# Mean of squares beside layer 3, expert banks freed by two engines, VectorE's masks and scans in another order, layer 5's relus on one engine

## The reference, cut to what matters

```python
# 1. mixer: 8 recurrent steps, in two directions
for _ in range(8):
    up   = relu(a + shift_r(up)   @ W2.T + b2)
    down = relu(a + shift_l(down) @ W2.T + b2)
h = relu(c + (shift_r(up) @ W4.T + b4) + (shift_l(down) @ W4.T + b4))
# 2. attention as a gated recurrence over 256 tokens, on layernorm(h)
#    (running maximum of log gates, decayed sums), then an RMS norm of its output
rms = sqrt(mean(out * out, axis=-1) + 1e-8)
h = h + out / rms * norm_scale
# 3. eight experts, each three 64x64 layers, mixed by a softmax over the batch mean
h = h + ffn(layernorm(h))
```

## Time and profile before

| | |
|---|---|
| median of 3 runs | 638.05 us (637.66 to 638.29) |
| the profiled execution: its own time | 636.97 us |
| its span, first to last instruction | 635.2 us |
| outside the span | 1.77 us |
| TensorE busy | 587.7 us, 93% |
| VectorE, ScalarE, GpSimd busy | 436.5, 344.4 and 123.1 us |
| mean granted TensorE clock | 0.967 of full speed |

### The profile page before, as it was taken

One profiled execution on the slowest core, in us unless ns is written; L12 is line 12 of the kernel. 1 busy time (PEld: TensorE's weight loads), 2 busy tenths in 40 slices (PEclk: granted clock), 3 DMA queues, 4 the chain that ended last, 5 costly groups with the idle time before them and its releaser, 6 DMA issues.

```text
span 635.2 us, 11790 instructions
## 1 busy us (share of the span) xinstructions
PE 587.7 (93%) x4731; PEld 229.5 (36%) x4731; DVE 436.5 (69%) x747; ACT 344.4 (54%) x608; POOL 123.1 (19%) x140
## 2 busy tenths in 40 slices
PE   6889998999999999999999999878799999999995
PEld 4323342334334334334334334233443333333331
DVE  2336864893895795797697598496237887776765
ACT  2238363754845854864854864887533344344441
POOL 9200020132113023015015015025011111010100
PEclk9989897999999989999989999999769999999998
DMA  1300000000000000000000000000001212211122
GB/s 41 90 3 2 1 3 0 1 2 3 2 1 3 2 1 3 1 2 4 1 1 1 1 2 2 1 1 1 6 1 18 34 19 33 35 24 27 21 32 33
DMA packets 37432, 7.27 MB, mean 11 GB/s; under 512 B 36405, under 2 KB 36701, under 8 KB 37373
## 3 DMA queue, kind: packets, MB, share of 16 engines
q1 hardware_dynamic: 36301, 5.72, 5.2%
q0 software_dynamic: 768, 0.69, 0.4%
q10 hardware_dynamic: 304, 0.07, 0.0%
HBM read 2.26 MB, written 4.19 MB: 10 GB/s over the span
## 4 chain that ended last, share of the span: by engine, by line
PE 76%; DVE 16%; issue 4%; ACT 3%; POOL 0%; DVEq 0%; POOLq 0%
PE TB L776 15%; PE TB L766 10%; PE QB L1117 7%; PE QB L799 7%; PE TB L893 6%; PE QB L826 5%; DVE M L1342 4%; PE TB L901 3%; PE QB L901 3%; PE QB L819 3%; PE TB L874 3%; PE QB L843 2%; DVE E L1516 2%; PE TB L826 2%; DVE XC_IS L1526 2%
## 5 line engine op out<-in xcount | busy, mean ns | idle before, releaser
L497 ACT ACTIVATE U<-TB 128x512 f32<-128x512 f32 x128 | 69.5, 596 | 132.4 <-PE TB L766 132.4
L776 PE MATMUL TB<-U,w2T 64*64 64x512 f32 x896 | 129.4, 615 | 8.3 <-ACT U L497 4.7
L718 ACT ACTIVATE E<-TB,bn_t 128x512 f32<-128x512 f32 x112 | 70.9, 684 | 92.8 <-PE TB L893 92.8
L1192 DVE TENSOR_SCALAR U<-TB 128x512 f32<-128x512 f32 x128 | 81.9, 681 | 54.1 <-PE TB L766 54.1
L766 PE MATMUL TB<-X,w_in 6*128 6x512 f32 x512 | 73.9, 647 | 2.1 <-DVE fw L1473 0.9
L893 PE MATMUL TB<-XN,fw 64*64 64x512 f32 x512 | 71.2, 611 | 4.0 <-issue 3.6
L776 PEld LDWEIGHTS TB<-U,w2T 64*64 64x64 f32 x896 | 43.5, 137 | 66.7 <-issue 29.5
L1117 PE MATMUL QB<-E,fwo 64*64 64x512 f32 x224 | 58.4, 593 | 2.3 <-DVE XC_IS L1526 1.7
L799 PE MATMUL QB<-XC_IS,wproj 64*64 64x512 f32 x384 | 56.5, 606 | 2.9 <-ACT LI L611 2.7
L1117 PE MATMUL QB<-E,fwo_sw 64*64 64x512 f32 x224 | 57.6, 593 | 0.0
L1516 DVE SCALAR_TENSOR_TENSOR E<-QB,t_neg,AT 128x512 f32<-128x512 f32 x54 | 38.0, 745 | 21.9 <-PE QB L901 21.9
(11 more groups left out here) (241 smaller groups left out, 904.7 us busy)
## 6 DMA issues: line engine op xcount, KB each, us to landing
result<-V SPq DMA_DIRECT2D x64, 64.0 KB, 1.8
X<-in_x SPq DMA_DIRECT2D x32, 8.0 KB
XN<-in_ffn_v SPq DMA_DIRECT2D x2, 256.0 KB, 3.6
XN<-in_ffn_g SPq DMA_DIRECT2D x2, 256.0 KB, 4.6
fw<-in_ffn_W POOLq DMA_DIRECT2D x2, 128.0 KB, 2.9
fw<-in_ffn_W POOLq DMA_DIRECT2D x2, 64.0 KB, 2.6
fwo<-in_ffn_Wo POOLq DMA_DIRECT2D x2, 64.0 KB, 2.6
fwo_sw<-in_ffn_Wo POOLq DMA_DIRECT2D x2, 64.0 KB, 2.3
```

What stands on the lines that cost most here:

```text
L497: nc.scalar.activation(U3[:, 2 * j:2 * j + 2, 1:T + 1], rowsof(TB[j][:, :]), ACT.Relu)\
L718: nc.scalar.activation(H1[i % 2][:, k, :], TB[k][:, :], ACT.Relu, bias=bn_t[:, 0, p:p + 1]).then_inc(b["h1"], 1)
L776: pe.matmul(TB[j][half[r ^ (j % 2)], :], w2T[half[r], D * r:D * r + D], U3[half[r], 2 * j:2 * j + 2, 2 * down:2 * down + T], start=True, s ...
L1192: nc.vector.tensor_scalar(U3[:, 2 * j:2 * j + 2, 1:T + 1], rowsof(TB[j][:, :]), 0.0, None, ALU.max)\
```

## The change

Four edits, all of the order of work or of who does it; the arithmetic stays.

1. In turns with mixer and late part, layer 3 is issued as bank 0, bank 1, the first half of the mean of squares, bank 3, the second half, bank 2; bank 2 is crossed there, and `turned` keeps account of which half holds which direction from then on. VectorE reads the mean of squares before its relus of layer 3 and no longer behind them.
2. The relus of layer 5 all run on ScalarE (`ON_ACT`), in every turn with a mixer; `relu_done` counts the semaphores accordingly.
3. VectorE's list in the middle of a turn: masks 0 and 1, scans 0 and 1, residual sum, masks 2 and 3, (no relu 5), scans 2 and 3, masks 4 and 5, then the normaliser.
4. In the experts VectorE frees only `QB[0]`; ScalarE copies `QB[1]` to a new tile `RQ` after its `h1`; GpSimd adds the two; the transposition comes one pair later. The last block is finished by VectorE alone, as before.

```diff
+ON_ACT = (5,)
+        RQ = [HR[:, 0:512], HR[:, 512:1024]]
+        SWAPPED = {(k, late): (1, 3) for k in range(1, 8) for late in (False, True)}
+        SWAPPED[3, True] = (1, 2, 3)
...
             for F in range(2 * G):
-                after(pool, b["res"], 2 * F - 3)
+                after(pool, b["res"], F - 1)
                 nc.gpsimd.tensor_tensor(rowsof(R1[F % 2]), rowsof(HH[:, HC * F:HC * F + HC]),
                                         BOW.unsqueeze(1).to_broadcast([P, 2, T]), ALU.add).then_inc(b["res_a"], 1)
+                if F > 0:
+                    pool.wait_ge(b["res"], F)
+                    pool.wait_ge(b["res_q"], F)
+                    nc.gpsimd.tensor_tensor(RES[(F - 1) % 2], RES[(F - 1) % 2], RQ[(F - 1) % 2], ALU.add)\
+                        .then_inc(b["res_sum"], 1)
...
-                for j in (0, 2):
+                for j in range(4) if k in ON_ACT else (0, 2):
...
             for i in range(N_PARKED + 1, len(made)):
                 h1(i)
+                F, p = made[i - 2] // EP, made[i - 2] % EP
+                if i > N_PARKED + 1 and p == EP - 1:
+                    act.wait_ge(b["l3_mm"], F + 1)
+                    after(act, b["res_sum"], F - 1)
+                    nc.scalar.activation(RQ[F % 2], QB[1][:, :], ACT.Identity).then_inc(b["res_q"], 1)
...
+            def layer(it, k, buf, late, beside=None):
+                if late and k == 3:
+                    bank_sum(it, k, 0, late)
+                    bank_sum(it, k, 1, late)
+                    for h, j in enumerate((3, 2)):
+                        beside(h)
+                        bank_sum(it, k, j, late)
...
                 if p == 0:
-                    after(pe, b["res"], 2 * F)
+                    after(pe, b["res"], F)
+                    after(pe, b["res_q"], F)
...
-                for j in (1, 3):
+                for j in () if k in ON_ACT else (1, 3):
...
                 nc.vector.tensor_tensor(RES[F % 2], QB[0][:, :], R1[F % 2], ALU.add).then_inc(b["res"], 1)
-                dve.wait_ge(b["res"], 2 * F + 1)
-                nc.vector.tensor_tensor(RES[F % 2], QB[1][:, :], RES[F % 2], ALU.add).then_inc(b["res"], 1)
...
-                if F >= 0 and behind == 1:
+                if F >= 0 and behind == 2:
                     token_major(F)
```

More of the change, by code:

```diff
@@ L254, in build @@
         ahead = {n: sem("ahead_" + n) for n in ("l1_mm", "h1", "l2_mm", "h2")}
+        SWAPPED = {(k, late): (1, 3) for k in range(1, 8) for late in (False, True)}
+        SWAPPED[3, True] = (1, 2, 3)
+        turned = {(j, k, late): sum(j in SWAPPED[i, late] for i in range(1, k)) % 2
+                  for j in range(4) for k in range(1, 9) for late in (False, True)}
         def settle(engine, it, mix, att, late):
@@ L767, in inputs, with bank_sum @@
                               start=(k == 0), stop=True).then_inc(s["mix_mm"], 1)
[L769 to L777, removed]
+            def bank_sum(it, k, j, late):
+                relu_done(pe, it, k - 1, j)
+                for r in range(2):
+                    down = r ^ turned[j, k, late]
+                    pe.matmul(TB[j][half[r ^ (j in SWAPPED[k, late])], :], w2T[half[r], D * r:D * r + D],
+                              U3[half[r], 2 * j:2 * j + 2, 2 * down:2 * down + T], start=True, stop=False)
+            def layer(it, k, buf, late, beside=None):
[5 more added lines that the diff above has]
+                        bank_sum(it, k, j, late)
+                else:
+                    for j in range(4):
+                        bank_sum(it, k, j, late)
                 inputs(it, k, buf)
@@ L943, in turn @@
                 if mix:
-                    layer(it, 1, buf)
+                    layer(it, 1, buf, late)
                 if att:
@@ L954, in turn @@
                 if mix:
-                    layer(it, 2, buf)
+                    layer(it, 2, buf, late)
                 if att and plain:
@@ L976, in turn @@
                 if mix:
-                    layer(it, 4, buf)
+                    layer(it, 4, buf, late)
                 if att and not plain:
@@ L983, in turn @@
                 if mix:
-                    layer(it, 5, buf)
+                    layer(it, 5, buf, late)
                 if late:
@@ L995, in turn @@
                 if mix:
-                    layer(it, 6, buf)
+                    layer(it, 6, buf, late)
                 if late:
@@ L1009, in turn @@
                 if mix:
-                    layer(it, 7, buf)
+                    layer(it, 7, buf, late)
                 if att and not plain:
@@ L1044, in turn @@
                 if mix:
-                    final(it, buf)
+                    final(it, buf, late)
                 if att and not plain:
@@ L1306, in turn @@
                             .then_inc(s["cs_out"], 1)
-                if mix:
-                    relu(it, 3)
                 if late:
@@ L1315, in turn @@
                             .then_inc(s["rms_add"], 1)
+                if mix:
+                    relu(it, 3)
                 if att and not plain:
@@ L1335, in turn, with running_max @@
                     relu(it, 4)
-                if att and not plain:
+                def running_max(ns):
                     dve.wait_ge(s["decay0_out"], a + 1)
                     after(dve, s["nq_out"], 2 * a)
-                    for n in range(SB):
+                    for n in ns:
                         dve.wait_ge(s["g_out"], 2 * a + n // 2 + 1)
@@ L1343, in turn @@
                             .then_inc(s["m_out"], 1)
+                if att and not plain:
+                    scores(a, range(0, 2))
+                    running_max(range(0, 2))
                 if last_late:
@@ L1361, in turn @@
                 if att and not plain:
-                    scores(a, range(0, 4))
+                    scores(a, range(2, 4))
                 if mix:
                     relu(it, 5)
+                if att and not plain:
+                    running_max(range(2, 4))
                 if att and not plain:
@@ L1368, in turn @@
                     dve.wait_ge(s["k_out"], 2 * a + 2)
+                    scores(a, range(4, 6))
                     for c in range(2):
@@ L1374, in turn @@
                         .then_inc(s["nn_first"], 1)
-                    scores(a, range(4, 6))
                     dve.wait_ge(s["lam_out"], a + 1)
```

41 lines of the change are left out of this document (28 added, 13 removed).

## The result

The median went from 637.86 us (four runs, 634.67 to 638.29) to **618.09 us** (four runs, 616.55 to 627.66); the ratio is 0.9692, with a 95% interval from 0.9644 to 0.9741. The prediction was 617.3 us, range 614 to 624. The profiled execution took 616.92 us, its span 615.1. One of the four runs, 627.66 us at a mean granted clock of 0.962 against 0.975 to 0.977 in the others, is not in the ratio.

A forecast was written before the change was run, and what follows sets the result against it. PE was taken as busiest, waiting for VectorE from relu 4 to layer 7 and for `finish` in experts. Terms 11.2 + 1.2 - 0.5 - 0.3 + 1.9 + 7.2 = 20.7 us gave 617.3 us, range 614 to 624.

The forecast's parts named there:

- 0.4 us a turn: Layers 3 to 4: sigmoid directly follows relu 3, so layer 4's inputs come 0.4 us sooner each turn; bounds 0 to 0.86.
- relu 6 starts 1.47 us sooner relative to relu 4: Middle of a turn: VectorE stays gapless, relu 6 moves 1.47 us sooner, and layer 7's inputs still follow 2.59 us later.
- The bounds: Edits 1 to 3, turns 2 to 7: 11.2 us forecast; 2.4 if only the 0.4 comes through, 16 with PE's freed time.
- 1.20 + 0.27: VectorE's list, relu 4 to relu 6: 1.20 us from two relus moved away, 0.27 from a first scan no longer slowed.
- the 1.9 us: Two half-clock stretches behind PE's 1.31 us idle time at the masks vanish, saving 2 x 0.94 us; bounds 0 to 1.9.
- The rival, falls elsewhere: Clock falls remain or two to four come anew around PE's other idle places, 0.94 us each: 619 to 623 us; chance 0.22.
- 0.3 lost: Turn 8, masks ahead of scans waiting for PE's scores, together with the last block's tail: 0.3 us lost.
- 0.5 forecast: Turn 0, mixer only: PE waits for every relu, two more in series on ScalarE cost 0 to 1.08 us; 0.5 lost.
- 7.2 us: Experts: the 0.48 us wait for `finish` vanishes in 15 of 16 blocks, 7.2 us in all; bounds 0 to 7.2.
- The slower rival: Experts: GpSimd's two adds a block hold up VectorE's weighted relus, 34 us more and the 7.2 gone: 658 us; chance 0.03.

The follow-up runs named there:

- e5: Changed kernel without edit 1, mean of squares behind layer 3 again: 627.22 us, ratio 0.9855 to the kernel before; full turns 48.08 us against 47.63.
- e6: Changed kernel with masks 4 and 5 back between the normaliser's first scan and the carry: 619.04 us, ratio 0.9732 to the kernel before; full turns 47.19 us.
- e3: Changed kernel with VectorE's masks and scans in the old order, layer 5's relus still on ScalarE: 625.38 us, ratio 0.9739 to the kernel before; full turns 48.00 us.
- e4: Changed kernel with layer 5's relus on ScalarE and VectorE again, new order kept: 629.08 us, ratio 0.9886 to the kernel before; full turns 48.62 us.
- after_again: Changed kernel measured again, unaltered, on one chip with e8 (repeated) and e9: 626.26 us, ratio 0.9852 to the kernel before.
- e2: Changed kernel with the experts of before (edits 1 to 3 alone): 626.26 us, ratio 0.9858 to the kernel before; full turns 47.62 us.
- e8: Changed kernel with the edits of e6 and e7 together: 617.44 us (ratio 0.9711 to the kernel before), repeated 614.76 us (0.9696); full turns 47.18 us.
- e7: Changed kernel with turn 0's relus of layer 5 on both engines: 620.73 us, ratio 0.9758 to the kernel before; turn 0 33.48 us.
- e9: e8 with the old order of masks and scans in turns without a mixer (turn 8): 614.23 us, ratio 0.9654 to the kernel before.

## Why the prediction was right, and where it was not

**Edit 1**: right in mechanism and size. 0.4 us a turn was put down to ScalarE's wait for projection 2; the wait is gone, 0.45 came, and e5 gives it back.

**Edits 2 and 3**: this step failed: "So VectorE again has no gap, relu 6 starts 1.47 us sooner relative to relu 4." It started 1.00 sooner. The two relus' 1.20 us came and the slow first scan went (0.68 us against 0.93, the pair at 264.75 taking 1.26). What was missed is what masks 4 and 5 did where they stood: they covered the normaliser's scan until the carry could read it, and they came late enough never to wait for their scores. Moved ahead, both joints open, each by 0.18 us (0.10 behind the predecessor's end in place of 0.08 ahead of it). e6 puts them back and gets 1.44 of the 1.47 in the turn. In turn 1 the same step cost 0.4: 47.76, and 47.35 with the masks put back. The bounds ran from 2.4 to 16 us and held it, yet nothing in the text asked what the moved masks had been hiding, though it asked that of everything else.

The Trainium skill (VectorE: DVE Perf Modes, "The DRAIN you can't avoid") says of eight copies, with a semaphore behind each or behind the last alone, that "the semaphore costs nothing extra here". In this case a wait for the predecessor's result does cost: the independent mask of e6 begins 0.08 us before the scan's end, the dependent carry of the kernel after 0.10 behind it. The same section says that an instruction which is not held starts before the pipeline behind the last one is empty; the 0.08 us agree with that.

The text also treated edits 2 and 3 as 1.20 + 0.27, two gains that add. They don't: 0.62 and 0.00 alone, 1.00 together. What the relus save comes through in full only if PE isn't held behind the masks (e3, where PE then sets the stretch), and PE's earlier start is of use only if VectorE's list has got shorter (e4, where PE waits 1.27 us for relu 6).

**The clock**: the 1.9 us came, and the four profiles against ten bear out the reason, PE's 1.31 us of idle time behind the masks; why this gap sets the fall off in one turn and not in the next is not explained by any run, and e4's 1.27 us in another place set off none. The rival, falls elsewhere, was right in turn 8 with one fall, and in executions that were not profiled it may have been right further: 619 to 623 was its price, and five of the six executions of after_again took 622 to 629. In turn 2 a stretch of 6.8 us (98.95 to 105.78 before) was missing from the profile after, 3.3 us that the sum didn't have; e2, whose turns are the same instructions, has it (6.8 us from 97.94, turn 2 57.70), so that it belongs to the execution and not to the change. Without that the span would have shrunk by 16.8 us, 3.9 less than forecast. That the median came within the range is luck in part: of the ten executions of the kernel after on record, 616.55 to 628.61 us, five are above 624.

**Turn 8**: forecast between 1 us either way, 0.3 lost taken; 1.0 was lost. The scans there did get shorter as hoped (3.27 us in two pairs against 4.49 in e3), but the mask ahead of them waits 1.14 us for its scores, and PE's idle time gathers in one piece with the fall behind it. The loss is the clock's: 3.4 us more at 0.50 than before in this part, and e8, which has the new order there but for masks 4 and 5 and as much half clock as before, loses nothing (85.3 against 85.6).

**Turn 0**: 0.47 lost, 0.5 forecast; e7 gives it back.

**Edit 4**: right. 6.9 of 7.2 us; the copy takes 0.60, fits, and PE has no wait. The slower rival had its mechanism and not its price: where GpSimd now adds, a stored pair's relus take 0.99 us on the mean in place of 0.73, the one beside the add 1.24 and the other 0.74; those from PSUM take 0.746 as before. The half microsecond a block is hidden in VectorE's spare time.

The Trainium skill's rule that was cited (SBUF — State Buffer, "Who interferes with whom"), that two SBUF inputs are held up by a GpSimd instruction that reads SBUF and a single one is not, agrees with the 1.24 and the 0.746 us.

## What to carry to other kernels

Before an instruction is moved out of a place, look at what stands to its left and right there: if its successor reads its predecessor's result, the moved instruction was the cover of that wait, and its removal costs the wait. Savings on two engines that feed each other in one stretch don't add; work out the stretch once with each alone and once with both. Where the granted clock moves from one execution to the next, take a change of under 1% from the lengths of undisturbed turns, and a total only beside the clock it ran at.

## What the runs showed of the hardware that was not expected

The same kernel on the same chip took 616.65 to 628.61 us, with the mean granted clock falling from 0.977 to 0.959 in step with the time. In the profiles the stretches at 0.50 in turns 0 to 2 come and go between executions of the same instructions: turn 0 takes 33.5 us without one and 35.0 with one (e9 and e8). What decides it at the start was not tried. In turns 3 to 7 the old order's stretches stand behind PE's 1.31 us of idle time at the masks, in one or two of five turns. In turn 8 a stretch stands behind a gap of 2.24 to 2.96 us in all nine profiles with the new order there, and in none of the five with the old one, whose gaps are 1.78, 1.31 and 0.43 us. From 430 us to the first `finish` the half clock lasts 10.2 to 23.9 us in these profiles; what sets its length no run shows.
